# A four-layer graph network: the last output unit moved into layer 3, and layer 0's late norm statistics made by ScalarE

## The chip, the core and the metric

The kernel is written in Bass for one core of a Trainium2 chip: TensorE (PE, with its weight loads as PEld), VectorE (DVE), ScalarE (ACT), GpSimd (POOL) and SyncE (SP), which only issues DMAs here. Each engine runs its own list of instructions in order, and they meet by semaphores. The metric is the device time of one execution in microseconds; lower is better. Line numbers (L1336) are those of the kernel before.

## The reference, cut to what matters

```python
# x: [16, 1024, 64], adj: [1024, 1024]; every layer: h = relu(layernorm(x)); x = x + f(h, adj)
# layer 0: Wh = h @ W; e = leaky_relu(s1[:, :, None] + s2[:, None, :]) + mask
#          x += elu(softmax(e, axis=2) @ Wh)
# layer 1: a softmax over neighbours for each channel
# layer 2: four heads of softmax(mask(h_k @ h_k.T)) @ h_k, cat, leaky_relu, @ Wo -> h2;
#          out2 = softmax(mask(h2 @ h2.T)) @ h2; x += layernorm(leaky_relu(out2)) * gamma + beta
# layer 3: the form of layer 0, with relu in place of elu
def _layernorm(x, axis=-1, eps=1e-5):
    m = jnp.mean(x, axis=axis, keepdims=True)
    v = jnp.var(x, axis=axis, keepdims=True)
    return (x - m) / jnp.sqrt(v + eps)
```

The matmuls of a layer can be counted in one unit of work: the attention of one batch (layers 0 and 3) or of one batch and head (layer 2), that is a 1024 x 1024 matrix of weights times a 1024 x 64 matrix of values.

## The kernel before

X stays in SBUF for all 16 batches. A batch's 1024 nodes lie in 8 blocks of 128, so a tile of X is 128 partitions by 8 blocks by 64 channels. Layers 0 and 3 have 16 units each (one a batch, `cur` in the code). Layer 2 has 80: per batch four heads and an output unit, in a list UNITS. The output unit of a batch comes inside the heads of the next; that of batch 15 (LAST) has no next batch and comes alone at the end. The unit ahead of it is head 3 of batch 15; the one ahead of that is head 2.

A unit has 8 steps `jt`. In layers 0 and 3, VectorE makes a 128x1024 tile of weights from S in PSUM (`gat_weights`, L1037) into a ring of 8, and TensorE sums it with the values (`weigh`, L1336). In layer 2 TensorE makes the dots (L1460), ScalarE the exponential (L874), VectorE the mask (L1174), and TensorE sums as before, three steps later. The sums of a unit gather in ACC, which ScalarE copies to `accs` (`gat_sums` or `sums`, L746) before the next unit may start to sum.

Each unit of layers 0 and 3 also prepares later batches: GpSimd normalizes batch cur+3 (`gat_norm`), TensorE turns it (`turn_norm`), ScalarE takes the relu (`h_relu`, L741); TensorE makes the node values and the S of batch cur+1 (`gat_nodes`), and ScalarE makes the factors from them (`gat_factors`, L769 to L783), for which it needs the two biases of GpSimd (`node_biases`, L575 and L577). In layer 0, the elu of the batch before is taken by ScalarE (`gat_below`, L759 and L761), VectorE (L1072) and GpSimd (`gat_add`, L561).

The statistics of the norm of layer 0 for batches 4 to 15 are made in units 0 to 11, for batch cur+4: VectorE sums (`stat_mean`, L1003 and L1005), GpSimd subtracts and squares (`stat_center`), VectorE sums again (`stat_var`, L1011 and L1013), and GpSimd raises to the power -0.5 (`stat_rstd`, L487). In units 2 to 9 GpSimd also makes an eighth of the mask with the diagonal (`add_diagonal`, L542 and L544), behind `stat_rstd` and `gat_add` and ahead of the next unit's `node_biases`.

Every order is written out by hand: nested loops with lines such as `if jt == 3 and late is not None: stat_var(layer, late)`. At the end of layer 2 TensorE, ScalarE and VectorE finish the unit before LAST, then turn its heads, make LAST's values and features (moved by eight DMAs of SyncE into FA), run LAST's 8 steps, and only then does layer 3 begin:

```python
                    if first == 0:
                        turn_heads(B - 1, 1)
                        values(LAST)
                        features(LAST)
                        spread_bound(LAST)
```

On GpSimd the end of layer 2 is `divide`, `values(LAST)`, `divide(LAST)`, `out_center`, `out_scale` (L709 to L717), and then `gat_norm(3, 0)`.

Of the kernel before, what the change touches and what calls it, by code (L numbers as in the profile page):

```python
# [11 lines left out]
P = 128  # L12
# [18 lines left out]
def gnn_stack(nc, x, adj, w_gat0, w_gat0_t, a_gat0, w0, b0, wa, ba, wh_t, bh, wo_t, bo, gamma, beta,  # L31
# [11 lines left out]
    with ExitStack() as ctx:  # L43
# [43 lines left out]
        st_x = sb("st_x", [P, 2, TD])  # L87
        ln_xc = sb("ln_xc", [P, TD])
# [123 lines left out]
        st_rstd_made = sem("st_rstd_made")  # L212
        y_made = sem("y_made")
# [65 lines left out]
        TILE0 = {0: 0, 2: B * T, 3: B * T * (2 + H)}  # L279
        UNIT0 = {0: 0, 2: B, 3: B * (2 + H)}  # L280
# [11 lines left out]
        def gat_buf(b):  # L292

            return 2 * (b % 2)
# [7 lines left out]
        LAST = UNITS[-1]  # L302
# [30 lines left out]
        def place_peak(layer, b):  # L333

            for half in range(2):
                place(("GF", layer, b, half), half)
            place(("GN", layer, b), 0)
# [6 lines left out]
        def place_gat(layer):  # L344

            place_norm(layer, 0)
            place_peak(layer, 0)
            place_nodes(layer, 0)
            place_norm(layer, 1)
            place_peak(layer, 1)  # L350
            place_norm(layer, 2)
            for cur in range(B):
                if cur + 1 < B:
                    place_nodes(layer, cur + 1)
                if cur + 2 < B:
                    place_peak(layer, cur + 2)
                if cur + 3 < B:
                    place_norm(layer, cur + 3)
# [19 lines left out]
        place_gat(0)  # L378
# [4 lines left out]
        for u in UNITS[:-1]:  # L383
# [6 lines left out]
            if is_head(u, 2) and u["b"] + 1 < B:  # L390
                place_norm(2, u["b"] + 1)
            if is_head(u, 3):
                place_pair("Z", u["b"], 0)
        place_pair("Z", B - 1, 2)
        place_values(LAST)
        place_features(LAST)
        place_bound(LAST)
        place_gat(3)

        def late_stats(layer, cur):  # L400
# [3 lines left out]
            return {1: B - 2, 3: B - 1}.get(cur)  # L404
# [56 lines left out]
        def _(pool):  # L461
# [11 lines left out]
            def stat_center(layer, b):  # L473

                n = G0[layer] + b
# [87 lines left out]
            def node_values(layer, b):  # L563

                n, buf = G0[layer] + b, gat_buf(b)
# [14 lines left out]
            def gat_layer(layer):  # L580
                if layer == 0:
                    stat_center(0, 0)
                    stat_rstd(0, 0)
                    gat_norm(0, 0)
                    stat_center(0, 1)
                    stat_center(0, 2)
                    node_biases(0, 0)
                    stat_rstd(0, 1, 2)
                    gat_norm(0, 1)
# [1003 lines left out]
```

## Time and profile before

| | |
|---|---|
| time, median of 3 runs | 2070.86 us (2069.59 to 2074.77) |
| the profiled execution | 2069.59 us, its span 2067.8 us |
| layer 0's units | about 37 to 246 us of the span |
| layer 1 | to about 462 us |
| layer 2 | about 462 to 1856 us, LAST from 1838 us on |
| layer 3's weights | 1883.6 to 2064 us |
| granted TensorE clock, mean | 0.975 |

The span is the time from the first instruction to the last; 1.8 us of the execution lie around it. Times in rows are microseconds from the start of the span. "Busy" adds the lengths of instructions. "Idle before" says what released the engine after a wait. A granted clock of 1.00 is 2.4 GHz and 0.50 is 1.2 GHz.

### The profile page before, as it was taken

Reading aid. Unit: us, or ns where it says so; the run is one execution under the profiler, and the core shown is the slowest. Engines: PE = TensorE matmul, PEld = TensorE weight load, DVE = VectorE, ACT = ScalarE, POOL = GpSimd, SP = SyncE. Lnnn points to the kernel's source line nnn. Section 1 sums busy time; section 2 is a strip of 40 time slices with the busy share of each in tenths; the row PEclk is TensorE's granted clock in tenths of the full one; section 3 lists DMA queues with packets and bytes.
Section 4 is the critical chain, followed back from the end, with each engine's and each line's share of the span. In section 5 each row is a group of like instructions: output and inputs, shape, how many; then the busy total and the mean of one; then the engine's idle time right before and its main releaser. Section 6 shows DMA issues by size and latency. Waiting matters only on the chain.

```text
span 2067.8 us, 94509 instructions
## 1 busy us (share of the span) xinstructions
PE 1925.2 (93%) x43528; PEld 1575.8 (76%) x43528; DVE 1695.6 (82%) x2052; ACT 1187.8 (57%) x1452; POOL 1060.0 (51%) x762
## 2 busy tenths in 40 slices
PE   5888789989999999999999999999999999966998
PEld 4777679987777777777777777777777777745887
DVE  5999878867788878888888888888888888845998
ACT  3444555516666666666666666666666666632342
POOL 6787688723244544545445454554545544335653
PEclk8999889999999999999999999999999999977999
DMA  6000000001111111111111111111111111100111
GB/s 175 4 3 4 3 2 2 2 12 33 34 33 33 34 33 33 33 34 33 33 33 34 33 33 33 33 34 33 33 34 33 34 33 33 33 12 8 24 30 34
DMA packets 88250, 61.19 MB, mean 30 GB/s; under 512 B 45616, under 2 KB 86832, under 8 KB 87856
## 3 DMA queue, kind: packets, MB, share of 16 engines
q1 hardware_dynamic: 85632, 54.57, 11.5%
q8 instruction: 342, 5.60, 1.1%
q10 hardware_dynamic: 2224, 0.59, 0.1%
q14 instruction: 52, 0.43, 0.1%
HBM read 8.98 MB, written 4.19 MB: 6 GB/s over the span
## 4 chain that ended last, share of the span: by engine, by line
PE 69%; DVE 15%; POOL 5%; ACT 4%; issue 3%; SPq 1%; DMA 1%; DVEq 0%; POOLq 0%; ACTq 0%
PE ACC L1336 30%; PE S L1460 23%; PE S L1439 5%; DVE ring L1174 4%; DVE ring L1037 4%; PE AX L1503 3%; PE AX L1512 2%; PE AX L1480 2%; POOL sp_log L660 1%; POOL ln_sq L663 1%; PE AX L1316 1%; PE S L1384 1%; PE AX L1326 1%; DVE ch_rden L1159 1%; ACT ring L874 1%
## 5 line engine op out<-in xcount | busy, mean ns | idle before, releaser
L1336 PEld LDWEIGHTS ACC<-V,ring 128*64 128x64 f32 x28672 | 965.0, 139 | 195.9 <-DVE ring L1037 67.3
L1174 DVE TENSOR_TENSOR ring<-ring,mask_self_t 128x1024 f32<-128x1024 f32 x640 | 891.2, 1402 | 195.5 <-ACT ring L874 191.5
L1336 PE MATMUL ACC<-V,ring 128*64 128x65 f32 x28672 | 989.0, 224 | 41.1 <-DVE ring L1037 34.1
L874 ACT ACTIVATE ring<-S,dot_bias 128x1024 f32<-128x1024 f32 x640 | 713.2, 1115 | 417.7 <-PE S L1460 380.1
L1460 PE MATMUL S<-FA 128*64 128x512 f16 x5120 | 667.1, 383 | 8.9 <-DMA FA<-lo 8.9
L1460 PEld LDWEIGHTS S<-FA 128*64 128x64 f16 x5120 | 254.4, 110 | 169.6 <-ACT ring L874 16.4
L1037 DVE SCALAR_TENSOR_TENSOR ring<-S,pair_q,mask_t 128x1024 f32<-128x1024 f32 x256 | 314.9, 1273 | 9.4 <-DVE f_max L1049 3.6
L676 POOL TENSOR_TENSOR EV_both<-score,recip 128x512 f32<-128x512 f32 x64 | 124.3, 1942 | 310.6 <-DVE score L1181 310.6
L1439 PE MATMUL S<-parts,mask_t 128*128 128x128 bf16 x3072 | 176.4, 221 | 13.7 <-DVE X L1163 13.6
L1439 PEld LDWEIGHTS S<-parts,mask_t 128*128 128x128 bf16 x3072 | 174.7, 99 | 15.5 <-issue 15.3
L746 ACT ACTIVATE accs<-ACC 128x520 f32<-128x520 f32 x112 | 66.9, 598 | 172.1 <-PE ACC L1336 172.1
L669 POOL TENSOR_TENSOR V<-v_pairs,bh_bc 128x512 f32<-128x512 f32 x64 | 96.5, 1508 | 120.6 <-ACT v_pairs L892 120.6
L526 POOL TENSOR_TENSOR ln_rstd<-ln_ve,neg_half 128x8 f32<-128x8 f32 x32 | 74.8, 2338 | 83.8 <-DVE ln_ve L1028 71.1
L676 POOL TENSOR_TENSOR relu_z<-score,recip 128x512 f32<-128x512 f32 x16 | 30.4, 1899 | 135.1 <-DVE score L1181 135.1
L892 ACT ACTIVATE v_pairs<-AX 128x512 f32<-128x512 f32 x80 | 47.8, 598 | 58.4 <-PE AX L1503 58.3
L517 POOL TENSOR_TENSOR ln_xc<-X,ln_mean 128x512 f32<-128x512 f32 x32 | 44.1, 1380 | 62.1 <-DVE ln_mean L1021 61.0
L487 POOL TENSOR_TENSOR st_rstd<-st_ve,neg_half 128x8 f32<-128x8 f32 (+1 forms) x31 | 65.5, 2114 | 9.6 <-DVE st_ve L1013 9.6
L1197 DVE TENSOR_REDUCE norm<-sq 128x8 f32<-128x512 f32 x80 | 54.1, 677 | 13.3 <-ACT sq L893 13.3
L569 POOL TENSOR_TENSOR V<-V 128x512 f32<-128x512 f32 x32 | 33.7, 1052 | 52.4 <-ACT V L775 51.5
L660 POOL TENSOR_TENSOR sp_log<-relu_z,on_mean 128x512 f32<-128x512 f32 x16 | 30.3, 1892 | 55.2 <-DVE on_mean L1215 55.2
L1159 DVE RECIPROCAL ch_rden<-S 128x512 f32<-128x512 f32 x16 | 53.6, 3348 | 5.8 <-PE S L1439 5.6
L1480 PE MATMUL AX<-ident,EV_both 128*128 128x128 f32 x256 | 35.2, 282 | 23.5 <-DVE norm_all L1205 19.1
(119 smaller groups left out, 1966.4 us busy)
## 6 DMA issues: line engine op xcount, KB each, us to landing
FA<-hi SPq DMA_DIRECT2D x320, 64.0 KB, 2.0
FA<-lo SPq DMA_DIRECT2D x320, 64.0 KB, 2.0
X<-in_x SPq DMA_DIRECT2D x16, 256.0 KB, 5.1
ring<-in_adj SPq DMA_DIRECT2D x8, 512.0 KB, 8.4
out_x<-X SPq DMA_DIRECT2D x16, 256.0 KB, 2.6
wh<-in_wh_t ACTq DMA_DIRECT2D x2, 64.0 KB, 6.8
bh_bc<-in_bh ACTq DMA_DIRECT2D x1, 128.0 KB, 10.0
w_gat<-in_w_gat ACTq DMA_DIRECT2D x4, 16.0 KB, 3.8
```

Of the source, the lines that this page charges most:

```text
L526: pool.tensor_tensor(ln_rstd[:, :], ln_ve[:, :], neg_half[:, 0:T], ALU.pow).then_inc(ln_pool, 1)
L669: pool.tensor_tensor(halves_of(V[:, u["n"] % 3, :, 1:D + 1]), v_pairs, halves_of(chans(bias)), ALU.add)\
L676: pool.tensor_tensor(dst, tiles(leaky[:, :]), cols(recip[:, :]), ALU.mult).then_inc(z_epi, 1)
L746: act.activation(accs_4d, acc_all, through).then_inc(acc_copied, 1)
L874: act.activation(ring[:, jt, :], S[jt % 2][:, :], ACT.Exp, bias=dot_bias[:, n % 2:n % 2 + 1])\
L1037: dve.scalar_tensor_tensor(out=ring[:, jt, :], in0=S[par][:, :], scalar=pair_q[:, par, jt:jt + 1], in1=mask_t[:, jt, :], op0=ALU.max, op1= ...
L1159: dve.reciprocal(tiles(ch_rden[:, :]), sums[:, :, D:2 * D]).then_inc(ch_recip, 1)
L1174: dve.tensor_tensor(ring[:, jt, :], ring[:, jt, :], mask_self_t[:, jt, :], ALU.mult)\
L1336: last = pe.matmul(acc_of(t)[rows, :], ring[:, jt, t * P + c * CUT:t * P + (c + 1) * CUT], values, start=(jt == 0 and t % 4 == 0), stop=(j ...
L1439: last = pe.matmul(S[par][:, t * P:(t + 1) * P], mask_t[:, j, t * P:(t + 1) * P], parts[:, par, part, j, :], start=(j == 0 and part == 0), ...
L1460: last = pe.matmul(S[jt % 2][rows, cut], FA[:, buf, 0, jt * P + c * CUT:jt * P + (c + 1) * CUT], FA[:, buf, i, cut], start=(i == 0), stop= ...
L1480: last = pe.transpose(AX[k][:, t * P:(t + 1) * P], z[:, row, chunk * P:(chunk + 1) * P], ident[:, :])
```

## The change

1. **LAST inside layer 3.** A constant FIRST = 2 places LAST between layer 3's units 1 and 2. Layer 3's first preparations (`gat_norm`, `turn_norm`, `gat_peak`, `gat_nodes`) are written between the steps of the unit ahead of LAST (BEFORE), LAST's values and features between the steps of layer 3's unit 1, and LAST's epilogue, mean, variance and addition between the steps of units 2 to 5. The statistics of layer 3's batch 15 go from unit 3 to unit 6. The numbering of units, of tiles and of PSUM banks follows.
2. **Layer 0's statistics of batches 4 to 15.** `stat_mean`, `stat_center` and `stat_var` are no longer called for them. ScalarE makes them in a new function at the end of its list of each of units 0 to 11: eight copies with an accumulating output, eight squares with one, and two small ones. `stat_rstd` waits for it.

```diff
+            def late_norm_sums(b):
+                par, n = b % 2, b - EARLY
+                act.wait_ge(x_in[b], 16)
+                if n == 0:
+                    act.wait_ge(st_var_made, 2 * EARLY)
+                wait(act, late_squared, T * n)
+                for t in range(T):
+                    act.activation(st_x[:, 0, t * D:(t + 1) * D], x_of(b)[:, t, :], ACT.Copy, scale=-1.0 / (8 * D),
+                                   accum_out=st_shift[:, par, t:t + 1]).then_inc(late_shifted, 1)
+                act.wait_ge(late_shifted, T * (n + 1))
+                for t in range(T):
+                    act.activation(st_x[:, 0, t * D:(t + 1) * D], x_of(b)[:, t, :], ACT.Square,
+                                   bias=st_shift[:, par, t:t + 1], scale=0.125,
+                                   accum_out=st_sum[:, par, t:t + 1]).then_inc(late_squared, 1)
+                act.activation(stat_of(st_mean, 0, b), st_shift[:, par, :], ACT.Copy, scale=-8.0).then_inc(late_ready, 1)
+                act.wait_ge(late_squared, T * (n + 1))
+                act.activation(stat_of(st_ve, 0, b), st_sum[:, par, :], ACT.Identity, bias=eps_c[:, :]).then_inc(late_ready, 1)
...
                     if cur > 0 and layer == 0:
                         gat_below(cur - 1)
                     if cur == 1 and layer == 0:
                         ranges()
+                    if late_stats(layer, cur) is not None:
+                        late_norm_sums(late_stats(layer, cur))
...
             def stat_rstd(layer, b, count=1):
-                pool.wait_ge(st_var_made, 2 * (G0[layer] + b + count))
+                if layer == 0 and b >= EARLY:
+                    pool.wait_ge(late_ready, 2 * (b - EARLY + 1))
+                else:
+                    pool.wait_ge(st_var_made, 2 * (stats_before(layer) + b + count))
...
             def dot_layer():                              # GpSimd
-                for u in UNITS[:-1]:
+                for u in UNITS[:-2]:
                     dot_unit(u)
-                divide(UNITS[LAST["n"] - 1])
-                values(LAST)
-                divide(LAST)
-                out_center(B - 1)
-                out_scale(B - 1)
+                gat_norm(3, 0)
+                gat_norm(3, 1)
+                divide(SECOND)
+                node_biases(3, 0)
+                out_scale(B - 2)
+                node_values(3, 0)
+                stat_rstd(3, B - 3)
+                gat_norm(3, 2)
...
+            def last_layer():                             # TensorE
+                for jt in range(T):
+                    gat_sums(3, 0, jt)
+                    if jt == 0:
+                        gat_nodes(3, 1)
+                    if jt == 2:
+                        gat_peak(3, 2)
+                    if jt == 5:
+                        turn_heads(B - 1, 1)
+                spread_peak(3, 2)
+                turn_norm(3, 3)
+                for jt in range(T):
+                    gat_sums(3, 1, jt)
+                    if jt == 0:
+                        gat_columns(3, FIRST)
+                    if jt == 1:
+                        values(LAST)
+                    if jt == 3:
+                        features(LAST)
+                    if jt == 5:
+                        spread_bound(LAST)
+                for jt in range(T + LAG):
+                    m = T * LAST["n"] + jt
+                    if jt < T:
+                        dots(m)
+                    if jt >= LAG:
+                        dot_sums(m - LAG)
+                    if jt == 1:
+                        gat_peak(3, FIRST + 1)
+                    if jt == 5:
+                        spread_peak(3, FIRST + 1)
+                    if jt == 6:
+                        turn_norm(3, FIRST + 2)
+                    if jt == T - 1:
+                        gat_gain(3, FIRST)
...
+            def last_layer():                             # VectorE
+                for jt in range(T):
+                    gat_weights(3, 0, jt)
+                    if jt == 0:
+                        node_max(3, 1)
+                    if jt == 2:
+                        node_peak(3, 1)
+                        epilogue(BEFORE)
+                    if jt == 5:
+                        node_max(3, 2)
+                    if jt == 6:
+                        out_add(B - 2)
+                for jt in range(T):
+                    gat_weights(3, 1, jt)
+                    if jt == 0:
+                        node_peak(3, 2)
+                        stat_mean(3, B - 2)
+                    if jt == 2:
+                        gat_reciprocal(3, 0)
+                    if jt == 4:
+                        norms(LAST)
+                    if jt == 5:
+                        feature_rest(LAST)
+                    if jt == 6:
+                        stat_var(3, B - 2)
+                    if jt == 7:
+                        bias(LAST)
```

`gat_columns` and `gat_gain` are the two halves of what was `gat_nodes` on TensorE and `gat_factors` on ScalarE: the node values, and S.

## Rows read from the trace of the kernel before

**Rows 1.** The page: busy time, share of the span and instructions of each engine.

```profile
PE 1925.2 (93%) x43528; PEld 1575.8 (76%) x43528; DVE 1695.6 (82%) x2052; ACT 1187.8 (57%) x1452; POOL 1060.0 (51%) x762
```

**Rows 2.** Busy time by stretch: stretch, its length, each engine, granted clock, DMA share, GB/s.

```profile
223.00:246.00 23.00, 14.18 (x348) 12.29 (x346) 20.28 (x29) 10.77 (x18) 13.67 (x14) 0.78 0.01 2
...
1818.00:1838.00 20.00, 7.50 (x92) 6.10 (x87) 3.71 (x8) 3.48 (x6) 5.84 (x5) 0.62 0.11 24
...
1856.00:1884.00 28.00, 8.80 (x124) 5.50 (x124) 5.49 (x14) 4.72 (x8) 16.56 (x18) 0.64 0.00 1
```

**Rows 3.** Timeline of ScalarE, layer 0: start, length, instruction, idle before.

```profile
187.29 0.60 ACT L746 ACTIVATE accs<-ACC 128x520 f32<-128x520 f32 x1 [5.79 <-PE ACC L1336]
...
200.38 0.60 ACT L746 ACTIVATE accs<-ACC 128x520 f32<-128x520 f32 x1 [5.80 <-PE ACC L1336]
...
203.86 0.31 ACT L775 ACTIVATE V<-f,node_bias 128x8 f32<-128x8 f32 x1 [0.24 <-ACT V L769]
204.07 0.29 ACT L777 ACTIVATE pair_q<-f,pair_bias 128x8 f32<-128x8 f32 x1
...
206.39 0.63 ACT L759 ACTIVATE below<-o 128x512 f32<-128x512 f32 x1
207.05 0.63 ACT L761 ACTIVATE below<-below 128x512 f32<-128x512 f32 x1
211.89 0.60 ACT L746 ACTIVATE accs<-ACC 128x520 f32<-128x520 f32 x1 [4.20 <-PE ACC L1336]
```

**Rows 4.** Timeline of VectorE in unit 11 of layer 0.

```profile
187.95 0.69 DVE L1003 TENSOR_REDUCE st_mean<-X 128x8 f32<-128x512 f32 x1
...
188.75 2.47 DVE L1037 SCALAR_TENSOR_TENSOR ring<-S,pair_q,mask_t 128x1024 f32<-128x1024 f32 x2
```

**Rows 5.** Timeline of ScalarE: its shortest instruction, of two columns.

```profile
61.12 0.20 ACT L795 ACTIVATE rng_log<-rng_abs 128x2 f32<-128x2 f32 x1
```

**Rows 6.** Timeline of GpSimd from unit 9 into unit 10 of layer 0.

```profile
169.20 1.65 POOL L487 TENSOR_TENSOR st_rstd<-st_ve,neg_half 128x8 f32<-128x8 f32 x1
171.81 1.27 POOL L561 TENSOR_TENSOR X<-X,o 128x512 f32<-128x512 f32 x1 [0.96 <-DVE o L1072]
173.02 1.03 POOL L542 COPY mask_self_t<-mask_t 128x1024 bf16<-128x1024 bf16 x1
174.21 0.29 POOL L544 TENSOR_SCALAR_AFFINE_SELECT mask_self_t<-mask_self_t 128x128 bf16<-128x128 bf16 x1
174.78 0.19 POOL L575 TENSOR_SCALAR node_bias<-f_peak 128x1 f32<-128x1 f32 x1 [0.28 <-DVE f_peak L1059]
```

**Rows 7.** Timeline of TensorE from the end of layer 2 into layer 3.

```profile
1814.29 4.04 PE L1336 MATMUL ACC<-V,ring 128*64 128x65 f32 x128
...
1838.83 5.95 PE L1460 MATMUL S<-FA 128*64 128x512 f16 x32 [6.72 <-DMA FA<-lo]
...
1845.55 1.03 PE L1460 MATMUL S<-FA 128*64 128x512 f16 x8
...
1847.34 1.03 PE L1460 MATMUL S<-FA 128*64 128x512 f16 x8
...
1885.00 2.00 PE L1336 MATMUL ACC<-V,ring 128*64 128x65 f32 x32 [0.98 <-DVE ring L1037]
...
1909.51 1.15 PE L1336 MATMUL ACC<-V,ring 128*64 128x65 f32 x32
...
1920.41 1.15 PE L1336 MATMUL ACC<-V,ring 128*64 128x65 f32 x32
```

**Rows 8.** Timeline of GpSimd at the end of layer 2: the scaling of batch 14.

```profile
1812.16 2.63 POOL L709 TENSOR_TENSOR on_rstd<-on_ve,neg_half 128x8 f32<-128x8 f32 x1
...
1818.32 1.26 POOL L717 TENSOR_TENSOR zt<-zt,beta_bc 128x512 f32<-128x512 f32 x1
```

**Rows 9.** Timeline of SyncE's queue: the first and last of LAST's eight DMAs.

```profile
1832.14 0.46 SPq L444 DMA_DIRECT2D FA<-hi  x1
...
1836.79 0.60 SPq L451 DMA_DIRECT2D FA<-lo  x1
```

More of the change, by code:

```diff
@@ L603, in gat_layer @@
                         node_biases(layer, cur + 1)
-                    if late is not None:
-                        stat_center(layer, late)
                     if cur + 1 < B:
@@ L624, in gat_layer, with first_last_units @@
                 gat_add(layer, B - 1)
+            def first_last_units():
+                node_biases(3, 1)
+                divide(BEFORE)
+                node_values(3, 1)
+                gat_norm(3, 3)
+                node_biases(3, 2)
+                node_values(3, 2)
+                values(LAST)
+                gat_divide(3, 0)
+                stat_center(3, B - 2)
+                gat_norm(3, 4)
+                stat_rstd(3, B - 2)
+                gat_add(3, 0)
+                gat_divide(3, 1)
+                gat_add(3, 1)
+            def last_layer():
+                for cur in range(FIRST, B):
+                    late = late_stats(3, cur)
+                    if cur + 1 < B:
+                        node_biases(3, cur + 1)
+                    if late is not None:
+                        stat_center(3, late)
+                    if cur + 1 < B:
+                        node_values(3, cur + 1)
+                    if cur == FIRST:
+                        divide(LAST)
+                    else:
+                        gat_divide(3, cur - 1)
+                    if cur + 3 < B:
+                        gat_norm(3, cur + 3)
+                    if late is not None:
+                        stat_rstd(3, late)
+                    if cur > FIRST:
+                        gat_add(3, cur - 1)
+                    if cur == FIRST + 1:
+                        out_center(B - 1)
+                    if cur == FIRST + 2:
+                        out_scale(B - 1)
+                gat_divide(3, B - 1)
+                gat_add(3, B - 1)
             def channel_step(k, par):
@@ L1097, in gat_layer @@
                     dve.wait_ge(mask_copied, T)
-                else:
-                    for b in range(2):
-                        node_max(layer, b)
-                        node_peak(layer, b)
                 for cur in range(B):
-                    late = late_stats(layer, cur)
                     for jt in range(T):
@@ L1107, in gat_layer @@
                             node_peak(layer, cur + 1)
-                        if jt == 0 and late is not None:
-                            stat_mean(layer, late)
                         if layer == 0 and cur == 0 and jt == 1:
@@ L1117, in gat_layer @@
                             gat_reciprocal(layer, cur - 1)
-                        if jt == 3 and late is not None:
-                            stat_var(layer, late)
                         if jt == 5 and cur + 2 < B:
@@ L1261, in dot_layer @@
                         dot_unit(u, jt)
[L1262 to L1270 removed]
+                        if u is BEFORE and jt == 1:
+                            node_max(3, 0)
+                        if u is BEFORE and jt == 2:
+                            node_peak(3, 0)
```

407 lines of the change are left out of this document (261 added, 146 removed).

## The prediction, made before the change was run

> **What bounds the kernel now.** I read the page first. TensorE is busy for 93% of the span and VectorE for 82% [rows 1], but these are means over stages with different limits, so I looked at the stages that the change touches: the timelines of layer 0 and of the passage from layer 2 to layer 3, and the busy time by stretch around both. I did not follow layers 1 and 2 further, since the change leaves their steps alone up to the last head.
>
> In layer 0 the distance of ScalarE's copy of the sums from one unit to the next is the period. It is 13.09 us in unit 11, the last that makes late statistics, and 11.51 us in unit 12, which makes none [rows 3]. Everything else in the two is alike. So VectorE, which spends 0.80 us on one of its two statistics steps (the start of the next instruction less the start of the sum [rows 4]), sets the period, and the late statistics cost 1.58 us a unit.
>
> From layer 2 to layer 3 nothing runs beside anything. Head 3 of batch 15 has its last sum at 1818.33, and the first sum of layer 3 is at 1885.00, 66.7 us later [rows 7], of which LAST's dots and sums take some 17. In the two stretches around LAST, TensorE is busy for 7.50 of 20 and 8.80 of 28 us at a granted clock of 0.62 and 0.64 [rows 2]. In steady layer 3 a unit takes 10.90 us, from sum to sum [rows 7], with TensorE nearly full.
>
> **Part 1, LAST inside layer 3.** I rebuild the passage from 1818.33 on. The unit BEFORE gets layer 3's first preparations between its steps, some 5 us of TensorE at full clock (four turns or spreads of 0.3 to 0.6, two peaks of 0.6, the node values 0.5, S 1.0), so its sums end at about 1821.3. ScalarE makes the factors of batch 0 behind its last exponential and ends at about 1821.4; VectorE then starts. But GpSimd must give TensorE the norm of batch 2 first: in its list this stands behind the head's division, the biases, the scaling of batch 14, the node values and the power. The scaling alone took 1812.16 to 1819.58, 7.4 us [rows 8]. With the others I get 1826, so layer 3's first sum is at about 1826.9: five us late, and VectorE is ahead by then.
>
> Unit 0 ends on TensorE at about 1838.4 (eight sums of 0.94 and 4 us of preparations and turned heads). In unit 1 LAST's chain runs through four engines: node values, ScalarE's copy, LAST's values on TensorE, ScalarE's copy, VectorE's norms, the turned values, ScalarE's `hi`, VectorE's `lo`. VectorE's norms stand at step 4 and `lo` at step 5 with the ring's weights queued behind them. I expect it to stand there for 3 to 4 us; `lo` is made at about 1847.1, and unit 1 ends on TensorE at about 1851.3. From the first issue of LAST's features to the dots it was 6.7 us before [rows 7, 9]: eight DMAs one behind the other and 2 us of landing. So the dots start at about 1853.5. LAST takes 18.6 us up to unit 2's first sum: 8 steps at 1.79 [rows 7], 14.3, three steps of lag, and S and factors for batch 2 at the end. Before, LAST's slow start (32 dots in 5.95 us [rows 7]) came on top; the clock should now be kept. Unit 2's first sum is then at 1872.1 against 1909.51 [rows 7]: 37.4 us earlier. From there the units are the same, except that VectorE has LAST's epilogue, mean, variance and addition in units 2 to 5 (four times about 0.75 us, where a unit has only 0.2 to 0.3 us to spare): 2.5 us back. Gain of part 1: **35 us**. Bounds: if all of TensorE's idle time and low clock in the two stretches went and nothing came back it would be some 43; if GpSimd's norm and LAST's chain stall for 10 us more, 25.
>
> **Part 2, the statistics on ScalarE.** It removes 1.58 us of VectorE and 2.2 us of GpSimd (`stat_center`) from each of units 0 to 11. If nothing took their place, the period would be 11.51.
>
> What it adds: 16 activations of 64 columns and two of 8 on ScalarE, called S below, in the gap of ScalarE in front of the copy of the sums. That gap is 4.20 us when the period is 11.51 [rows 3]; the other 7.3 us are ScalarE's own work with its waits on TensorE, which follow from the copy and do not shrink.
>
> No row shows an accumulating output, so I bound S. The main instruction: 0.204 us for two columns [rows 5] and 0.63 for 512 [rows 3] give 0.84 ns a column, so 0.26 for 64; with a column as bias, by the row of 0.29 for eight columns, 0.33. Instructions without a wait between them start before the end of the one ahead: 204.07 less 203.86 is 0.21 for a length of 0.31 [rows 3]. That takes 0.09 off each: 0.165 and 0.24. So 8 x 0.165 + 8 x 0.24 + two waits on its own last result and two small ones (0.55) make 3.8 us. The accumulator must then be written out, and I take that for an instruction of its own, as short as ScalarE's instructions come: between 0 (free) and 0.31 (0.20, with the overlap of 0.09 lost and 0.02 between the two). I take 0.20, the shortest length and also the shortest distance of starts here, since a read has to wait for the sum before it but can overlap what follows. S = 3.8 + 16 x 0.20 = **7.0 us**, bounds 3.8 and 8.8.
>
> Beside this the Trainium skill, "ScalarE: Activation LUTs", section "What ACT_TABLE_LOAD costs", gives 186 ns plus 0.833 ns a column, 93 ns more for a pointer operand, and 93 ns of overlap; the rows agree. It prices no accumulator read; by it alone, an estimate, S would be 3.7. The same page's rules for kernel authors put additions and products on VectorE, not on ScalarE, which speaks against the move.
>
> Two loops then compete with the period of 11.51.
> - ScalarE alone: 7.3 + S = 14.3 us.
> - Through GpSimd. `stat_rstd` now waits for the end of S, and behind it in GpSimd's list stand `gat_add`, the diagonal of units 2 to 9, and the next unit's biases, for which ScalarE's factors (L775) wait. From GpSimd's rows [rows 6]: 1.62 + 1.21 + 1.19 + 0.25 (starts to starts, waits taken off) + 0.27 + 0.19 and the hops make 4.9 us from the end of S to L775. From L775 to the end of L761 it is 3.8 [rows 3], of which 0.1 is overlapped. The loop is 8.65 + S = 15.65 us with the diagonal, 7.2 + S without.
>
> Against 13.09: units 3 to 10, which wait behind a diagonal, lose 8 x 2.56 = 20.5 us; units 1 and 11 lose 1.2 each. Unit 0 has a longer gap, and unit 2 has VectorE's range work of some 3 us, which now lies beside ScalarE: I put these at -1 together. That is 22. Then the clock: with a period of 15.65 and 10.9 us of TensorE's work, TensorE stands still for 4.7 us in each unit. In the tail of layer 0, with gaps of 3 to 4 us, the granted clock was 0.78 on the mean [rows 2], part of it at 1.2 GHz. The first sum and the node values would be slower after each gap; most of that hides behind GpSimd's 4.9 us, and I charge 3 us in all. Loss of part 2: **25 us**. With S = 3.8 it would be a gain: 8 x 0.64 + 4 x 1.58 = 11 us; with S = 8.8 a loss of 45. Each us of S is worth 11 us.
>
> **Sum.** -35 + 25 = -10 us. The profiled execution took 2069.59 us, its span 2067.8; so 2059.6, and as the median of the runs is 1.3 us above that execution, **2061 us**.
>
> **The rivals.**
> - *The read is nearly free* (S of 3.8 to 6.2). For it: the overlap of short instructions in the rows. Against it: something must be written out after the last element. At S = 5.4 the loops are 14.05 and 12.7, layer 0 loses 7, and the time is about 2042; at the end of it 2025. Chance 0.25. The page's prices without a read are this case; that it leaves out the read is why I do not follow it.
> - *The read stops the pipeline* (S from 7.8 to 9). This one ends on the other side: at S = 8.8 layer 0 costs 45 us, and the time is 2081. It decides from S = 7.9 on, where both parts cancel. For it: an instruction that waits for its own engine's last result shows no overlap in the rows (L759 to L761: 0.66 for 0.63). Chance 0.22.
> - *LAST stalls inside layer 3.* Its features pass through four engines with layer 3's weights queued behind each wait. If VectorE stands for 10 us instead of 4, and GpSimd is late for batch 3 as well, part 1 gives 20: 2076. Against it: the chain's parts are short and the ring holds eight tiles. Chance 0.08.
> - The forecast keeps 0.45, with a range of its own of 2050 to 2070.
>
> **How the numbers follow.** A measurement of this kernel tells 0.3%, 6.2 us, from no change. Faster than 2064.6: most of the forecast (0.33) and the first rival (0.25). Within: the rest of the forecast and the lower ends of the others, 0.20. Slower: 0.22. The range of 2033 to 2081 leaves out the lowest third of the first rival and the top of the second.
>
> **What the profile will show.** Right: in layer 0 the copy of the sums at a distance of about 15.6 us in units 3 to 10 and 14.3 in unit 11, no idle time in front of it, L575 waiting for nothing but GpSimd's own list, rows of accumulator reads of about 0.2 us on ScalarE; VectorE waiting in layer 0 for ScalarE's S. In the passage, the first sum of layer 3 near 1827 less the shift of layer 0, LAST's dots waiting for the DMA of `lo`, and the granted clock near 1.00. Wrong: a period of 11.5 in layer 0 (S was small and GpSimd's chain shorter than I think), or a gap of over 10 us around LAST.

## The result, and the profile after

The changed kernel takes 2045.1 us (median of 4 runs, 2043.08 to 2047.2); the kernel before, run beside it, 2071.7 (2069.59 to 2074.77). The ratio is 0.9871, with a 95% interval of 0.9853 to 0.9888. The profiled execution took 2043.08 us, its span 2041.3, at a mean granted clock of 0.984. That is 26.6 us less than before where I forecast 10 less: the sign was right, and the time lies in the range of 2033 to 2081, but 15.9 us below the forecast of 2061 and outside the likeliest case's own 2050 to 2070.

The page, first part: busy time of each engine. Against [rows 1], ScalarE has 58 us and 408 instructions more, VectorE and GpSimd have less.

```profile
PE 1908.1 (93%) x43528; PEld 1565.7 (77%) x43528; DVE 1686.4 (83%) x2005; ACT 1245.5 (61%) x1860; POOL 1035.0 (51%) x738
```

**Layer 0.** The timeline of ScalarE from unit 5's copy of the sums to the factors behind unit 6's copy (start, length, instruction, idle before; L847 is now the copy of the sums, L867 and L871 the new sums, L902 the factor that waits for GpSimd):

```profile
117.86 0.58 ACT L847 ACTIVATE accs<-ACC 128x520 f32<-128x520 f32 x1
...
126.72 0.24 ACT L867 ACTIVATE st_x<-X 128x64 f32<-128x64 f32 x1
126.86 0.19 ACT L867 ACTIVATION_READ_ACCUMULATOR st_x<-X 128x1 f32 x1
126.96 0.24 ACT L867 ACTIVATE st_x<-X 128x64 f32<-128x64 f32 x1
...
129.10 0.33 ACT L871 ACTIVATE st_x<-X,st_shift 128x64 f32<-128x64 f32 x1
...
129.43 0.33 ACT L871 ACTIVATE st_x<-X,st_shift 128x64 f32<-128x64 f32 x1
...
131.76 0.58 ACT L847 ACTIVATE accs<-ACC 128x520 f32<-128x520 f32 x1
...
134.37 0.60 ACT L896 ACTIVATE V<-AX 128x512 f32<-128x512 f32 x1 [1.54 <-PE AX L1589]
136.88 0.31 ACT L902 ACTIVATE V<-f,node_bias 128x8 f32<-128x8 f32 x1 [1.91 <-POOL pair_bias L639]
```

Three things stand here. The copy of the sums no longer waits (5.79 us of idle time before it in [rows 3]); the distance from copy to copy is 13.90 us. The accumulator is read by an instruction of its own, 0.19 us long, but the next activation starts 0.24 us after the one before (0.33 for a square), so a read takes less room than its length. And S is 131.76 less 126.72 = 5.04 us, not 7.0. The last row shows who sets the period: ScalarE's factor waits for GpSimd's second bias. GpSimd's timeline from the end of S:

```profile
131.93 1.65 POOL L549 TENSOR_TENSOR st_rstd<-st_ve,neg_half 128x8 f32<-128x8 f32 x1 [4.25 <-ACT st_ve L876]
133.54 1.27 POOL L623 TENSOR_TENSOR X<-X,o 128x512 f32<-128x512 f32 x1
134.76 1.04 POOL L604 COPY mask_self_t<-mask_t 128x1024 bf16<-128x1024 bf16 x1
135.95 0.29 POOL L606 TENSOR_SCALAR_AFFINE_SELECT mask_self_t<-mask_self_t 128x128 bf16<-128x128 bf16 x1
136.32 0.19 POOL L637 TENSOR_SCALAR node_bias<-f_peak 128x1 f32<-128x1 f32 x1
136.59 0.19 POOL L639 TENSOR_SCALAR pair_bias<-f_peak 128x1 f32<-128x1 f32 x1
```

This is the loop through GpSimd as the prediction drew it, 5.1 us from the end of S to L902 where it said 4.9. The starts of all copies of the sums, in ordinary figures:

| unit | 0 | 1 | 2 | 10 | 11 | 12 | 13 |
|---|---|---|---|---|---|---|---|
| before | 53.26 | 66.70 | 82.54 | 187.29 | 200.38 | 211.89 | 223.39 |
| after | 50.79 | 63.70 | 76.18 | 187.32 | 199.79 | 211.18 | 222.68 |

From unit 2's copy to unit 10's, eight units, it is 104.75 us before and 111.14 after: 6.4 lost. Units 0, 1, 2 and 11 gain 2.5, 0.5, 3.4 and 0.6. By these starts layer 0 is 0.7 us shorter. But they count from the start of the span, and ScalarE's copy of the node values ahead of unit 0 began at 41.84 before and at 41.50 after; in the traces of the other kernels below it began anywhere from 40.96 to 43.76. Counted from it, unit 0 gains 2.1 us, and up to unit 11's copy it is 158.5 us before and 158.3 after.

**The passage.** TensorE's timeline (L1729 dots, L1548 sums, L1528 the turn of a normalized batch):

```profile
1797.66 1.03 PE L1729 MATMUL S<-FA 128*64 128x512 f16 x8
...
1804.79 1.04 PE L1528 MATMUL AX<-ident,ln_y 128*128 128x128 f32 x4 [5.16 <-POOL ln_y L568]
1805.76 1.92 PE L1729 MATMUL S<-FA 128*64 128x512 f16 x8
1807.46 1.50 PE L1548 MATMUL ACC<-V,ring 128*64 128x65 f32 x32
...
1829.24 0.44 PE L1538 MATMUL AX<-ident,f_max 128*64 128x128 f32 x4 [1.28 <-DVEq L1210]
1832.68 1.11 PE L1528 MATMUL AX<-ident,ln_y 128*128 128x128 f32 x4 [3.00 <-POOL ln_y L568]
1833.72 2.00 PE L1548 MATMUL ACC<-V,ring 128*64 128x65 f32 x32
...
1861.20 1.92 PE L1729 MATMUL S<-FA 128*64 128x512 f16 x16 [0.96 <-DMA FA<-lo]
...
1879.47 1.15 PE L1548 MATMUL ACC<-V,ring 128*64 128x65 f32 x32 [0.85 <-DVE ring L1195]
```

The long gap of [rows 7] is gone: unit 2 of layer 3 begins to sum at 1879.47 instead of 1909.51. But ahead of it, after the first step of BEFORE, TensorE now stands for 5.16 us, which I had not foreseen, and its next dots and sums take 1.92 and 1.50 instead of 1.03 and 1.10. The releaser is GpSimd's norm; its timeline shows what it did meanwhile:

```profile
1798.62 1.95 POOL L759 TENSOR_TENSOR sp_log<-relu_z,on_mean 128x512 f32<-128x512 f32 x1 [3.10 <-DVE on_mean L1370]
1800.65 1.90 POOL L762 TENSOR_TENSOR ln_sq<-sp_log 128x512 f32<-128x512 f32 x1
1802.51 1.04 POOL L561 TENSOR_TENSOR ln_xc<-X,st_mean 128x512 f32<-128x512 f32 x1
1803.69 1.04 POOL L568 TENSOR_TENSOR ln_y<-ln_xc,st_rstd 128x512 f32<-128x512 f32 x1
```

L759 and L762 are `out_center` of batch 14, which waits for VectorE's mean. Behind it in GpSimd's list stands the first norm of layer 3, although nothing that the norm needs is late. Busy time by stretch (columns as in [rows 2]) for layer 0's slow units and for the two stretches that hold the stops:

```profile
59.00:161.00 102.00, 82.27 (x2474) 71.21 (x2471) 87.64 (x103) 78.11 (x335) 60.43 (x69) 1.00 0.01 3
...
1790.00:1820.00 30.00, 24.84 (x494) 18.93 (x490) 19.36 (x28) 13.68 (x15) 12.12 (x9) 0.94 0.08 20
1820.00:1850.00 30.00, 25.41 (x696) 21.45 (x692) 20.24 (x27) 13.96 (x23) 17.53 (x19) 0.94 0.01 3
```

The granted clock is 1.00 in layer 0, so a period of 13.9 us costs no clock. In the two stretches of the passage it is 0.94, against 0.62 and 0.64 in those around LAST before [rows 2]. During LAST itself, from 1861 to 1879 us, it is 1.00.

### The profile page after: what moved, and what is told of

It is laid out like the page before. It is cut to its first block, busy times and chain, and to the rows that moved or that the text cites. A ratio compares the mean times of both kernels' runs of the same rounds, so it can differ in the third digit from the quotient of the medians.

```text
span 2041.3 us, 94849 instructions
## 1 busy us (share of the span) xinstructions
PE 1908.1 (93%) x43528; PEld 1565.7 (77%) x43528; DVE 1686.4 (83%) x2005; ACT 1245.5 (61%) x1860; POOL 1035.0 (51%) x738
## 4 chain that ended last, share of the span: by engine, by line
PE 68%; DVE 13%; ACT 8%; POOL 6%; issue 3%; DMA 1%; SPq 1%; ACTq 0%; POOLq 0%; DVEq 0%
PE ACC L1548 29%; PE S L1729 23%; PE S L1708 5%; DVE ring L1327 4%; PE AX L1772 3%; DVE ring L1195 2%; PE AX L1781 2%; PE AX L1749 2%; POOL sp_log L759 1%; POOL ln_sq L762 1%; ACT st_x L871 1%; PE AX L1528 1%; DVE ch_rden L1312 1%; ACT ring L1001 1%; PE AX L1538 1%
## 5 line engine op out<-in xcount | busy, mean ns | idle before, releaser
L1548 PEld LDWEIGHTS ACC<-V,ring 128*64 128x64 f32 x28672 | 961.5, 139 | 205.4 <-DVE ring L1195 53.7
L1548 PE MATMUL ACC<-V,ring 128*64 128x65 f32 x28672 | 981.0, 224 | 53.5 <-DVE ring L1195 35.0
L1729 PE MATMUL S<-FA 128*64 128x512 f16 x5120 | 666.1, 382 | 2.1 <-DMA FA<-lo 2.1
L1729 PEld LDWEIGHTS S<-FA 128*64 128x64 f16 x5120 | 253.6, 110 | 161.8 <-ACT ring L1001 15.8
L1708 PEld LDWEIGHTS S<-parts,mask_t 128*128 128x128 bf16 x3072 | 174.4, 99 | 15.6 <-issue 15.4
L847 ACT ACTIVATE accs<-ACC 128x520 f32<-128x520 f32 x112 | 66.7, 595 | 95.7 <-PE ACC L1548 95.7
L759 POOL TENSOR_TENSOR sp_log<-relu_z,on_mean 128x512 f32<-128x512 f32 x16 | 30.4, 1900 | 54.2 <-DVE on_mean L1370 54.2
L1344 DVE TENSOR_TENSOR lo<-AX,hi 128x512 f16<-128x512 f32 x80 | 54.6, 683 | 1.1 <-ACT hi L1035 1.1
```

The source lines that it names most:

```text
L847: act.activation(accs_4d, acc_all, through).then_inc(acc_copied, 1)
L1548: last = pe.matmul(acc_of(t)[rows, :], ring[:, jt, t * P + c * CUT:t * P + (c + 1) * CUT], values, start=(jt == 0 and t % 4 == 0), stop=(j ...
L1708: last = pe.matmul(S[par][:, t * P:(t + 1) * P], mask_t[:, j, t * P:(t + 1) * P], parts[:, par, part, j, :], start=(j == 0 and part == 0), ...
L1729: last = pe.matmul(S[jt % 2][rows, cut], FA[:, buf, 0, jt * P + c * CUT:jt * P + (c + 1) * CUT], FA[:, buf, i, cut], start=(i == 0), stop= ...
```

## The experiments

A time is the median of 4 to 11 runs, a ratio is to the kernel before on the same chip, with its 95% interval in brackets. "After" is the changed kernel, 2045.1 us. Differences to it are of medians from different chips; the median of the kernel before lay between 2069.9 and 2071.7 us on them.

**One part at a time.** The first kernel is the changed one with `stat_mean`, `stat_center` and `stat_var` of batches 4 to 15 back on VectorE and GpSimd. The second is the kernel before with `late_norm_sums` and its wait in `stat_rstd` alone.

```diff
 # e_part1, from after
-                    if late_stats(layer, cur) is not None:
-                        late_norm_sums(late_stats(layer, cur))
...
 # e_part2, from before
+                    if layer == 0 and late_stats(layer, cur) is not None:
+                        late_norm_sums(late_stats(layer, cur))
...
-                    if late is not None:
+                    if late is not None and layer == 3:
                         stat_center(layer, late)
```

> The changed kernel with part 2 undone: layer 0's late statistics are VectorE's and GpSimd's again, LAST stays inside layer 3. Theory A (both terms of my sum were too large in size: part 1 gave some 25 us, part 2 about nothing): period of layer 0 back at 13.09 us, time 2045 to 2048. Theory B (part 1 gave 35 us as predicted and part 2 cost some 9): 2036 to 2038. Theory C (part 2 was a gain of some 10 us and part 1 gave 15): 2055.

> The kernel before with part 2 alone. Theory A: layer 0's copies of the sums at 13.9 us in units 3 to 10 and about 12.5 in units 1, 2 and 11, the sum of both within 2 us of before: 2069 to 2072. Theory B: 2080. Theory C: 2061.

Measured: part 1 alone 2048.28 us, 0.9882 (0.9868 to 0.9895), 23.3 less than before on its chip. Part 2 alone 2072.0 us, 0.9996 (0.9988 to 1.0005): no change. Added, the two give -22.9, and together they gave -26.6; the intervals, of 1.8 to 3.6 us to each side, allow that. So both terms of my sum were too large: 35 should be 23 to 27, and 25 should be nothing, or a gain of up to 3.

The traces agree. With part 1 alone layer 0's copies of the sums lie 13.09 us apart again. With part 2 alone they lie 13.9 apart in units 3 to 10 and 12.48 in units 2 and 11, and from the node values to unit 11's copy it is 158.4 us, beside 158.5 before and 158.3 after. Part 1 alone starts layer 3 no later than after does, counted from BEFORE's first dots, but then stays longer at a low clock: LAST's first 16 dots take 3.59 us instead of 1.92, and unit 2's first sum comes 84.8 us behind BEFORE's first dots instead of 81.8. That is most of the 3.7 us by which the whole exceeds the sum, though one execution of each doesn't settle it. TensorE's timeline with part 1 alone:

```profile
1802.78 1.03 PE L1731 MATMUL S<-FA 128*64 128x512 f16 x8
...
1867.67 3.59 PE L1731 MATMUL S<-FA 128*64 128x512 f16 x16 [0.95 <-DMA FA<-lo]
...
1887.54 1.15 PE L1550 MATMUL ACC<-V,ring 128*64 128x65 f32 x32 [0.86 <-DVE ring L1192]
```

**Where part 1 lost 12 us.** Two kernels move one norm each on GpSimd, a third both. `gat_norm(3, 0)` goes ahead of `out_center(14)`, into the list of the unit SECOND; `gat_norm(3, 2)` goes ahead of `out_scale(14)` and the power.

```diff
 # e_norm0
+                if u is SECOND:
+                    gat_norm(3, 0)
...
-                gat_norm(3, 0)
                 gat_norm(3, 1)
 # e_norm2 (e_norms has both)
                 node_biases(3, 0)
-                out_scale(B - 2)
+                gat_norm(3, 2)
                 node_values(3, 0)
+                out_scale(B - 2)
                 stat_rstd(3, B - 3)
-                gat_norm(3, 2)
```

> The changed kernel with GpSimd's norm of layer 3's batch 0 moved one unit up, ahead of the centring of batch 14, where GpSimd waits 3.1 us anyway. Theory A: TensorE's stop of 5.16 us in the unit ahead of LAST, and the half clock behind it (dots of 1.85 us in place of 0.87, a sum of 1.5), come from that norm alone; both go, 6 to 7 us less: 2038 to 2039. Theory B: the time comes back at the next wait, since GpSimd's list up to the norm of batch 2 stays as long: the first sum of layer 3 moves by under 2 us and the time is 2043 or more.

> The changed kernel with GpSimd's norm of layer 3's batch 2 ahead of the scaling of batch 14. Theory A: TensorE's stops of 1.28 and 3.00 us ahead of layer 3's first sum shrink to under 1.5 in all and the half clock behind them goes: 4 to 6 us less, 2039 to 2041. Theory B: the scaling, now later, holds VectorE's addition of batch 14 and the norms behind it, and gives most of it back in unit 0: 2043 to 2045.

> Both of these moves together. If they are two separate stops, the gains add up: 10 to 13 us less than the changed kernel, 2032 to 2035, and part 1 alone is then worth what I had predicted for it, 35 us. If they are one chain through GpSimd, the pair gives no more than the larger of the two.

Measured: 2038.69 us, 0.9843 (0.9828 to 0.9858) for the first, 6.4 us under after; 2043.11, 0.9857 (0.9836 to 0.9878) for the second, 2.0 under; 2033.99, 0.9821 (0.9806 to 0.9836) for both, 11.1 under. TensorE's timeline with both norms early:

```profile
1797.64 1.03 PE L1730 MATMUL S<-FA 128*64 128x512 f16 x8
...
1800.12 1.05 PE L1730 MATMUL S<-FA 128*64 128x512 f16 x8
...
1823.33 1.15 PE L1549 MATMUL ACC<-V,ring 128*64 128x65 f32 x32
1825.21 0.69 PE L1590 MATMUL AX<-w_gat,h_t 64*64 64x64 f32 x32 [0.72 <-DVEq L1220]
...
1869.10 1.15 PE L1549 MATMUL ACC<-V,ring 128*64 128x65 f32 x32 [0.85 <-DVE ring L1196]
```

BEFORE's first dots start within 0.02 us of after's, so the two timelines can be laid side by side. Step 1's dots come at 1800.12 instead of 1805.76 (5.64 earlier: the stop), the first sum of layer 3 at 1823.33 instead of 1833.72 (10.4), unit 2's at 1869.10 instead of 1879.47 (10.4). The predictions of 1826.9 and 1872.1, less the 1.8 us by which everything ahead had moved, are 1825.1 and 1870.3: with both norms early the passage is within 2 us of what I had drawn. With only the first one early, the stop of 5.16 is gone and those of 1.28 and 3.00 remain. The second norm alone gave 2.0 us, less than half of the 4 to 6 of my theory A; its time is one that theory B gave, but its trace doesn't show what B says. VectorE's addition of batch 14 waits for nothing, and from layer 3's first sum to unit 2's it takes 45.7 us as in after. The stop of 3.00 is gone, and unit 2's first sum comes 2.4 us earlier, counted from BEFORE's first dots. Its stop of 5.16 us is still there, and the low clock behind it lasts longer than in after: the sum and the dots that follow take 1.94 and 1.66 us instead of 1.50 and 1.03. Its four runs spread over 5.5 us, so the single figure is not to be read closely.

**Is the loop through GpSimd what sets layer 0's period?** In this kernel `stat_rstd` runs one unit later, between `gat_divide` and `gat_norm`, where GpSimd has time; nothing else is moved.

```diff
+                    if cur > 0 and late_stats(layer, cur - 1) is not None:
+                        stat_rstd(layer, late_stats(layer, cur - 1))
                     if cur + 3 < B:
                         gat_norm(layer, cur + 3)
-                    if late is not None:
-                        stat_rstd(layer, late)
```

> The changed kernel with GpSimd's power for batch cur+4 moved from the end of unit cur to just ahead of the norm that needs it, in unit cur+1, behind the next biases and node values. If the loop through GpSimd (end of the statistics, power, addition, diagonal, biases, ScalarE's factors) sets the 13.89 us, the period of units 3 to 10 falls to the 12.3 to 12.5 that units 1, 2 and 11 have, 8 x 1.4 = 11 us less: about 2034. If ScalarE's own list or its waits on TensorE set the 13.89, nothing changes: 2045.

Measured: 2036.22 us, 0.9818 (0.9803 to 0.9833). ScalarE's timeline, two copies of the sums and the factor between them:

```profile
102.71 0.58 ACT L847 ACTIVATE accs<-ACC 128x520 f32<-128x520 f32 x1
...
106.17 0.31 ACT L902 ACTIVATE V<-f,node_bias 128x8 f32<-128x8 f32 x1 [0.24 <-ACT V L896]
...
114.93 0.58 ACT L847 ACTIVATE accs<-ACC 128x520 f32<-128x520 f32 x1
```

The factor no longer waits for GpSimd, and the period is 12.22 us. ScalarE alone is then the loop: the prediction's 7.3 + S, with S = 5.04, is 12.34. Unit 11's copy comes 11.2 us earlier than in after, the end 8.9 by the medians and 7.5 by the two traces. Of the difference 2.5 us lie in layer 2: from its first to its last turn of `norm_max` it takes 1330.8 us in the trace of after and 1333.3 here, but also 1331.8 in that of the kernel before and 1334.3 in that of part 1 alone. What makes layer 2 differ by a few us between executions was not tried.

**What a longer S costs.** The eight copies are made twice, which adds 8 x 0.24 = 1.9 us to S and brings it to the 7.0 that I had predicted.

```diff
-                act.wait_ge(late_shifted, T * (n + 1))
+                act.wait_ge(late_shifted, 2 * T * n + T)
+                for t in range(T):
+                    act.activation(st_x[:, 0, t * D:(t + 1) * D], x_of(b)[:, t, :], ACT.Copy, scale=-1.0 / (8 * D),
+                                   accum_out=st_shift[:, par, t:t + 1]).then_inc(late_shifted, 1)
+                act.wait_ge(late_shifted, 2 * T * (n + 1))
```

> The changed kernel with the eight copies of each late batch made twice (the second time over the first, same values). ScalarE's late statistics grow by 8 x 0.24 and a wait, about 2.0 us. If they lie on the loop in every one of units 1 to 11, the time grows by 22 to 24 us to about 2068; if half is hidden, by 11.

Measured: 2073.57 us, 1.0007 (0.9998 to 1.0016), 28.5 us over after, which is more than the 22 to 24 that I expected. S is 7.09 us in its trace (123.41 to the copy at 130.50), and units 3 to 10 have a mean period of 15.97, where the prediction's 8.65 + 7.0 is 15.65 and after's own 8.85 + 7.09 is 15.94. Its busy time by stretch, and the copy of the node values behind a copy of the sums:

```profile
59.00:200.00 141.00, 110.81 (x2907) 92.58 (x2903) 102.31 (x120) 108.72 (x531) 73.20 (x85) 0.87 0.01 3
...
118.46 0.60 ACT L900 ACTIVATE V<-AX 128x512 f32<-128x512 f32 x1 [2.83 <-PE AX L1593]
```

At this period the clock does fall, to 0.87 on the mean of the stretch, and the wait for the node values grows from 1.54 to 2.83 us. This kernel is the world of the prediction: from the node values to unit 11's copy it takes 184.1 us, 25.5 more than before, and by the times part 2 would cost 25 to 29, where I had said 25. The model of layer 0 held, and its input was wrong.

**Is it the read that costs, or the activations?** The same activations without the accumulating output. The statistics of batches 4 to 15 are left out; constants stand in their place.

```diff
-                    act.activation(st_x[:, 0, t * D:(t + 1) * D], x_of(b)[:, t, :], ACT.Copy, scale=-1.0 / (8 * D),
-                                   accum_out=st_shift[:, par, t:t + 1]).then_inc(late_shifted, 1)
+                    act.activation(st_x[:, 0, t * D:(t + 1) * D], x_of(b)[:, t, :], ACT.Copy, scale=-1.0 / (8 * D))\
+                        .then_inc(late_shifted, 1)
...
```

> The changed kernel with the 16 activations of a late batch left without their accumulating output, so the statistics of batches 4 to 15 in layer 0 are constants written at the start (shift 0, sum 1) and not computed; all waits and all other work stay. It prices the accumulator's write-out alone. By the starts in the profile of the changed kernel a read adds 0.095 us: 16 of them 1.5 us. Theory A (the loop through GpSimd holds, 8.85 us and the statistics): units 3 to 10 at 12.4 in place of 13.89, units 1 and 11 at VectorE's 11.5: 14 to 16 us less, about 2030. Theory B (the reads are hidden behind the next instruction's start): 2045, nothing changes.

Measured: 2027.79 us, 0.9798 (0.9784 to 0.9813), 17.3 less than after, a little more than the 14 to 16 expected. ScalarE's timeline:

```profile
120.32 1.26 ACT L867 ACTIVATE st_x<-X 128x64 f32<-128x64 f32 x8
121.61 2.02 ACT L871 ACTIVATE st_x<-X,st_shift 128x64 f32<-128x64 f32 x8
...
123.67 0.30 ACT L876 ACTIVATE st_ve<-st_sum,eps_c 128x8 f32<-128x8 f32 x1
```

From the first copy to L876 it is 3.35 us; in after it is 131.55 less 126.72 = 4.83. The difference over 16 reads is 0.093 us each. A read is 0.19 us long and takes half of that.

Beside this the Trainium skill, "ScalarE: Activation LUTs", section "What ACT_TABLE_LOAD costs": its 186 ns plus 0.833 ns a column, and 93 ns for a pointer operand, give 0.24 and 0.33 us for 64 columns, and the trace agrees with both (0.24 and 0.33). It gives no price for the read.

**Versions beyond the change.** With the norms early and the power late together:

> The two norms moved and GpSimd's power of the late statistics moved as well. The three edits lie in different stages and should add up: some 9 to 10 us from layer 0 and 10 to 13 from the passage, about 2023 to 2026.

Measured: 2022.22 us, 0.9766 (0.9751 to 0.978), just under what I expected. Then S itself was cut. The variance is taken as mean square less squared mean, so that the squares need no bias and wait for nothing, and ScalarE's two small activations fall away; two VectorE instructions of 8 columns take their place, first behind step 3.

```diff
 # e_plain, from e_all
+            def late_var(b):
...
+                dve.tensor_tensor(st_shift[:, par, :], own, own, ALU.mult).then_inc(late_ready, 1)
+                dve.wait_ge(late_ready, 2 * n + 1)
+                dve.scalar_tensor_tensor(out=stat_of(st_ve, 0, b), in0=st_sum[:, par, :], scalar=EPS,
+                                         in1=st_shift[:, par, :], op0=ALU.add, op1=ALU.subtract).then_inc(late_ready, 1)
...
+                        if jt == 3 and cur > 0 and late_stats(0, cur - 1) is not None:
+                            late_var(late_stats(0, cur - 1))
 # e_plain_jt1
+                        if jt == 1 and cur > 0 and late_stats(0, cur - 1) is not None:
 # e_pool_var: the small ones on GpSimd, ahead of its power
+                    pool.tensor_tensor(st_shift[:, par, :], own, own, ALU.mult).then_inc(late_ready, 1)
...
+                    pool.tensor_tensor(stat_of(st_ve, 0, b), st_sum[:, par, :], st_shift[:, par, :], ALU.subtract)\
...
+                    pool.tensor_scalar(stat_of(st_ve, 0, b), stat_of(st_ve, 0, b), 1.0, EPS, ALU.mult, ALU.add)\
...
```

> The last combination (both norms and the power moved) with the variance as the mean square less the square of the mean: the squares need no shift, so no bias operand and no wait between copies and squares, and the two small activations go; VectorE gets two instructions of eight columns for each late batch. ScalarE's statistics fall from 5.0 to some 3.9 us, its list to 11.1, and VectorE's 11.5 and 0.25 set the period: 11.7 to 11.8 in place of 12.23, about 5 us less, 2016 to 2018. If VectorE's two small ones cost as much as a whole statistics step (0.8), the period is 12.3 and the time stays at 2022.

Measured: 2031.24 us, 0.9816 (0.98 to 0.9832), 9 us slower than without it, where I had expected 5 us less or no change, with a period of 13.09. The timelines of VectorE and of GpSimd show why:

```profile
108.31 0.68 DVE L1175 TENSOR_TENSOR st_shift<-st_mean 128x8 f32<-128x8 f32 x1
109.02 0.96 DVE L1177 SCALAR_TENSOR_TENSOR st_ve<-st_sum,st_shift 128x8 f32<-128x8 f32 x1
```

```profile
107.92 1.04 POOL L631 TENSOR_TENSOR V<-V 128x512 f32<-128x512 f32 x1 [2.87 <-ACT V L898]
108.92 1.04 POOL L615 TENSOR_TENSOR o<-accs,recip 128x512 f32<-128x512 f32 x1
```

Instructions of 8 columns take 0.68 and 0.96 us, and each ends with the GpSimd instruction that was running when it started: 108.99 beside 108.96, 109.98 beside 109.96. So it is with 23 of the 24 in layer 0, which end 0.02 to 0.04 us behind GpSimd's; the 24th started with GpSimd idle and took 0.17. I had priced them by their columns alone. The next kernel puts the same two behind step 1, where GpSimd does nothing.

> The mean-square kernel with VectorE's two small instructions of eight columns two steps earlier, behind step 1 of the next unit in place of step 3. Behind step 3 they took 0.68 and 0.96 us, and each ended just as a GpSimd instruction did (the node values, the division). Behind step 1 GpSimd is idle, waiting for ScalarE. Theory A (a VectorE instruction with two SBUF inputs stands until GpSimd's current one is done): both take about 0.2, the period falls from 13.10 to 11.7 or 11.8, and the time is 2015 to 2018. Theory B (they cost that much anywhere, by themselves): period and time stay, 2031.

The timeline of VectorE, the same two lines:

```profile
104.94 0.16 DVE L1175 TENSOR_TENSOR st_shift<-st_mean 128x8 f32<-128x8 f32 x1
105.13 0.17 DVE L1177 SCALAR_TENSOR_TENSOR st_ve<-st_sum,st_shift 128x8 f32<-128x8 f32 x1
```

They take 0.16 and 0.17 us; the period is 11.77 and the time 2017.12 us, 0.9746 (0.9731 to 0.976). The last kernel takes them off VectorE.

> The mean-square kernel with these small instructions on GpSimd instead (a product, a difference, the addition of the epsilon, each of eight columns, just ahead of the power). VectorE is left with 11.5 us a unit and ScalarE's list with 11.1, GpSimd has room. Period 11.5 to 11.6, 2012 to 2015. If GpSimd's three short ones delay the division or the norm so that ScalarE's relu or the turn waits, 12 and more.

Measured: 2012.07 us, 0.9724 (0.9707 to 0.974), with a period of 11.50, that of the units without statistics. This beats both kernels, the changed one by 33 us. Two of the copies of the sums on ScalarE's timeline:

```profile
111.65 0.61 ACT L858 ACTIVATE accs<-ACC 128x520 f32<-128x520 f32 x1 [0.37 <-PE ACC L1554]
...
123.15 0.61 ACT L858 ACTIVATE accs<-ACC 128x520 f32<-128x520 f32 x1 [0.38 <-PE ACC L1554]
```

The copy of the sums waits for TensorE again, for 0.38 us: ScalarE makes its sums in the gap and is no longer what sets the period.

## Why the prediction was right in sign and wrong in size

**Part 1, the term of 35.** Measured 23.3 by itself. In the trace of both parts layer 3's unit 2 came 28.2 us earlier, once the 1.8 us from ahead are taken off, against 37.4 predicted, and 3.5 us were given back behind it against 2.5. The 1.8 us are no part of either term: layer 0 began 0.3 us earlier in that execution, part 2 gave 0.2, and the rest came in layers 1 and 2, where executions differ anyway. The step that failed is "BEFORE gets layer 3's first preparations between its steps, some 5 us of TensorE". I priced the preparations on TensorE and asked of GpSimd only when it would be ready with the norm of batch 2; I did not ask the same of batch 0's norm, which stands behind `out_center(14)` and its wait of 3.10 us for VectorE's mean. That is 5.16 us of stop and 1.3 us of slow dots and sums after it. The rest of the 8.6 us by which layer 3's first sum was late, 2.1, is put down to GpSimd's list behind it, which gave batch 2's norm later than I had summed (the stop of 3.00, part of which I had allowed for). With both norms early part 1 is worth 23.3 + 11.1 = 34.4 us by the sum of two differences (the two norms early without part 2 were not run), so apart from GpSimd's order the passage was sized rightly: from layer 3's first sum to unit 2's, over units 0 and 1 and LAST, it took 45.75 us where I had 45.2, and LAST's dots waited for the DMA of `lo` as said. VectorE stood for 0.65 us ahead of LAST's norms and not at all ahead of `lo`, where I had 3 to 4. The rival in which part 1 gives 20 named the right engine but the wrong batch: it had GpSimd late for batch 3, and GpSimd was late for batch 0 and then for batch 2.

**Part 2, the term of 25.** Measured nothing alone (0.4 us more, by the ratio 0.8 less, both within the noise), and a gain of 3.3 beside part 1. The step that failed is "I take 0.20" for the read. Its length was right (0.19), but I argued that a read "has to wait for the sum before it" and added its whole length; it overlaps both neighbours and takes 0.093. Sixteen reads are 1.5 us instead of 3.2, and the activations themselves 3.5 instead of 3.8: S was 5.04 instead of 7.0.

The two loops were right: 8.85 + S through GpSimd against 8.65 + S, shown by taking the power out of it and, with an S of 7.09, by the kernel with the copies made twice; 7.2 + S on ScalarE against 7.3 + S. (Two terms of the first were read a little low: [rows 6] give 1.65 and 0.29 for 1.62 and 0.25.) At its "Each us of S is worth 11 us" the missing 1.96 us are 21.6 of the 25, and the 3 us charged for the clock did not come, since at 13.9 us the clock stays at 1.00. In the same terms, unit by unit: units 3 to 10 lost 6.4 instead of 20.5, units 1 and 11 gained 1.1 instead of losing 2.4, units 0 and 2 gained 5.5 instead of 1, and the clock cost 0 instead of 3; together 25.1 us, from the 25 lost to the 0.2 gained. Unit 2's gain is ScalarE's loop again: 12.48 us with part 2, as in unit 11, and 15.84 without it, in both pairs of kernels. Of unit 0's 2.1, 0.8 lie ahead of it, where GpSimd's biases come sooner; the rest was not traced. What was measured is the first rival, "the read is nearly free", to which I gave 0.25: S lies in its middle, though with this S its own sum has layer 0 lose some 3 us, and layer 0 gained 0.2.

**The sum.** -35 + 25 = -10 held two errors of opposite sign, 8 to 12 us in part 1 and 25 to 28 in part 2. The first cancelled part of the second, and this is luck: with part 1 at its predicted 35 the same layer 0 would have given some 2034 to 2037 us, near the lower edge of the range. The result of -26.6 lies near the first rival's -29, but part of that nearness is the same cancelling: that rival still had part 1 at 35 and layer 0 losing 7.

**Of what the profile was to show:** no idle time in front of the copy of the sums, read rows of about 0.2 us, LAST's dots waiting for `lo` and a clock near 1.00 in LAST came; the distances of 15.6 and 14.3 us (13.9 and 12.5) and the first sum near 1825 (1833.7) did not. Nor did VectorE wait for ScalarE's S in layer 0: its longest wait in units 3 to 10 is 1.2 us, for `below` (L883).

## What to carry to other kernels

When work is written between the steps of a unit, follow every engine's list for the first item as well as for the last: a short step that waits for another engine holds up whatever stands behind it in its list, even if that needs nothing late. A cost that is multiplied by a loop of a dozen units needs its unknown sized by what it adds from start to start, not by the length of its row. And when a step becomes the end of a loop through several engines, look for a place one unit later for the part that nobody needs yet; that and the two norms were worth 23 us here.

## What the runs showed of the hardware

- In the trace of after, ScalarE's accumulating output shows as an instruction of its own, 0.19 us long. From start to start a pair on 64 columns takes 0.24 us, or 0.33 with a column as bias, and against the kernel without the output that is 0.093 us for each read.
- VectorE's two instructions of 8 columns, both with two inputs in SBUF, ended when GpSimd's ended if they started while GpSimd ran one on SBUF (23 of 24): 0.68 and 0.96 us where it is 0.16 and 0.17 with GpSimd idle. The Trainium skill, "SBUF — State Buffer", section "Who interferes with whom", says that such an instruction contends with a GpSimd instruction that reads SBUF, and that the later one blocks; this trace agrees, and in all 23 cases VectorE was the later one. Here it multiplied the cost by four to six.
- In layer 0 the granted clock was 1.00 (2.4 GHz) with a period of 13.9 us and 0.87 on the mean with one of 15.97. Behind the one stop of 5.16 us in BEFORE, eight dots took 1.92 us instead of 1.03; the next eight took 1.03 again in after and 1.66 in the kernel with the second norm early.
